# Scan of the delta rule: gathered rows in two buffers, TensorE's small products spread over VectorE's solution, products of the identity in what is left

## The reference, cut to what matters

```python
def step(M, inp):
    q_t, k_t, v_t, b_t = inp
    out_t = einsum('bnh,bnhd->bnd', q_t, M)
    retrieved = einsum('bnhd,bnd->bnh', M, k_t)
    delta = v_t - retrieved
    M = M + b_t[..., None, None] * einsum('bnh,bnd->bnhd', k_t, delta)
    return (M, out_t)
...
_, outs = jax.lax.scan(step, M0, xs)
...
rms = sqrt(mean(out * out, axis=-1) + EPS)
return (out / rms * rms_weight) @ Wo.T
```

## Time and profile before

| | |
|---|---|
| median of 3 runs | 2787.47 us (2787.09 to 2791.15) |
| the profiled execution's own time | 2809.05 us |
| its span, first to last instruction | 2807.4 us |
| mean granted TensorE clock | 0.925 of full speed |
| PE busy | 2337.0 us (83%) |
| DVE busy | 1622.4 us (58%) |
| ACT busy | 1364.7 us (49%) |
| POOL busy | 1143.1 us (41%) |

### The profile page before, as it was taken

How to read it: one execution, slowest core, us unless ns; L and a number is a source line. 1 busy time by engine, 2 the same in 40 slices (tenths; PEclk the granted TensorE clock), 3 DMA queues, 4 the chain that set the end, 5 groups by cost and what they waited for, 6 DMA issues and landing times. The chain is left out here.

```text
span 2807.4 us, 55147 instructions
## 1 busy us (share of the span) xinstructions
PE 2337.0 (83%) x20480; PEld 1593.8 (57%) x20480; DVE 1622.4 (58%) x4120; ACT 1364.7 (49%) x2098; POOL 1143.1 (41%) x1179
## 2 busy tenths in 40 slices
PE   5955566666999888888888887999789879999977
PEld 3534455555666454555455454676556756666666
DVE  4666777766113567767766763432254346877753
ACT  3531222222332386877787685533111347777752
POOL 3319999970001266646645653000076003223220
PEclk9977898877999899999999999999799989999999
DMA  4454445531101021111111111000000100000001
GB/s 147 150 147 147 140 137 156 155 110 52 37 1 36 29 66 48 59 44 54 57 56 39 52 51 46 0 1 0 2 1 1 36 0 1 1 1 1 1 1 60
DMA packets 158461, 149.00 MB, mean 53 GB/s; under 512 B 21169, under 2 KB 141105, under 8 KB 155121
## 3 DMA queue, kind: packets, MB, share of 16 engines
q1 hardware_dynamic: 138432, 105.51, 12.7%
q0 software_dynamic: 3456, 23.07, 2.4%
q10 hardware_dynamic: 16304, 16.83, 2.0%
HBM read 100.51 MB, written 40.63 MB: 50 GB/s over the span
## 5 line engine op out<-in xcount | busy, mean ns | idle before, releaser
L1633 POOL TENSOR_SCALAR a_dist<-a_dist,a_mq 128x512 f32<-128x512 f32 x512 | 354.9, 721 | 161.0 <-ACT a_mq L1572 161.0
L1676 DVE TENSOR_SCALAR_CACHE_REDUCE a_dist<-a_ring 128x512 f32<-128x512 f32 x512 | 332.3, 686 | 103.8 <-PE a_ring L1321 102.4
L1562 ACT ACTIVATE a_pT<-a_psT 128x1024 f32<-128x1024 f32 x256 | 257.9, 1023 | 123.6 <-PE a_psT L1333 116.5
L1333 PE MATMUL a_psT<-ident,a_dist 128*128 128x128 f32 x2048 | 276.2, 284 | 17.7 <-ACT a_pT L1562 17.6
L1333 PEld LDWEIGHTS a_psT<-ident,a_dist 128*128 128x128 f32 x2048 | 244.4, 146 | 50.6 <-issue 21.2
L1556 ACT ACTIVATE a_dist<-a_dist 128x2048 f32<-128x2048 f32 x128 | 237.0, 1902 | 61.5 <-DVE a_dist L1676 58.6
L1321 PE MATMUL a_ring<-a_stack 102*128 102x512 bf16 x512 | 190.3, 409 | 78.8 <-DVE a_dist L1676 42.4
L1321 PEld LDWEIGHTS a_ring<-a_stack 102*128 102x128 bf16 x512 | 48.5, 99 | 253.1 <-DVE a_dist L1676 174.7
L1002 POOL TENSOR_TENSOR c_y<-c_prod 128x1024 f32<-128x1024 f32 x16 | 37.2, 2349 | 335.6 <-DVE c_prod L1035 333.7
L3050 ACT ACTIVATE ds_wtm<-ds_wg,ds_par 128x256 f32<-128x256 f32 x64 | 29.0, 501 | 266.4 <-DVE ds_wg L3184 225.7
L1346 PE MATMUL a_psO<-a_pT,a_va 128*32 128x512 f32 x1024 | 143.9, 640 | 2.3 <-ACT a_pT L1562 2.3
(11 more groups left out here) (404 smaller groups left out, 5490.6 us busy)
## 6 DMA issues: line engine op xcount, KB each, us to landing
a_stack<-a_parts_dram SPq DMA_DIRECT2D x384, 64.0 KB
a_parts_dram<-a_parts SPq DMA_DIRECT2D x32, 384.0 KB, 2.5
bf_w<-in_up_w_dram POOLq DMA_DIRECT2D x10, 1024.0 KB, 5.8
bf_w<-in_down_w_dram POOLq DMA_DIRECT2D x10, 1024.0 KB, 6.9
ds_nbg<-tok_nbk ACTq DMA_DIRECT2D x128, 64.0 KB
X<-in_x_dram SPq DMA_DIRECT2D x2, 2048.0 KB, 11.1
feat_v<-di_part SPq DMA_DIRECT2D x16, 256.0 KB, 2.6
tok_nbk<-di_nbk SPq DMA_DIRECT2D x16, 256.0 KB, 2.9
```

Source lines behind the costliest of these rows:

```text
L1333: last = turn(psT[:, u % 2, kb, q * P:(q + 1) * P], dist[:, g % 2, i, q, k * P:(k + 1) * P], core.ident[:])
L1562: a(pT[:, u // 2, u % 2], psT[:, u % 2], ACT.Exp).then_inc(exp_done, 1)
L1633: last = nc.gpsimd.tensor_scalar(d, d, -1.0, mq[:, g % 2, i, q:q + 1], ALU.mult, ALU.add)
L1676: ts(dist[:, gg % 2, i, q, :], ps[:], 1e-12, 3.0e38, ALU.max, ALU.min, accum_out=mq[:, gg % 2, i, q:q + 1]).then_inc(ring_out, 1)
```

## The change: what it does

- nbg gets two buffers and two semaphores. ScalarE issues the load for chunk n + 1 in the middle of chunk n (after `root`), where it waits only for the previous chunk's products, which read that buffer.
- On TensorE `tile` moves ahead of `products` and waits for the sixth instruction of the solution; where there is no tile yet (j = 0), `fill(3)` stands there. `products` waits for the 14th. Behind L2966 comes a new `fill(3)` that waits for the 19th. `fill(3)` is three products of the identity with two copies of the identity (128 x 128 by 256 columns) into psX, which is written anew before it is read again.
- On ScalarE `take_out` moves ahead of the copies into pb, `tile_ready` ahead of `keys`, and `root` and the loads of nbg ahead of the load of qj.

```diff
+        PER = 3 * (CT // 2 - 2) + 4
-        nbg = sbf("nbg", [P, G, G, P])
+        nbg = sbf("nbg", [P, 2, G, G, P])
...
+            def fill(n):
+                for _ in range(n):
+                    mm(psX.rearrange("p j g t -> p (j g t)"), core.ident[:],
+                       core.ident[:].unsqueeze(1).broadcast_to([P, 2, P]), start=True, stop=True, skip_group_check=True)
...
                 last.then_inc(w_ps, 1)
 
+                ch.wait(pe, sol, PER, 4 + 6)
+                if ch.j:
+                    tile(Chunk(ch.j - 1, ch.pp, ch.u), 0, 0)
+                else:
+                    fill(3)
+
+                ch.wait(pe, sol, PER, 4 + 14)
                 if more:
                     products(ch.next())
-
                 ch.wait(pe, m2_done, 1, 1)
...
                 last.then_inc(o1_ps, 1)
 
-                if ch.j:
-                    tile(Chunk(ch.j - 1, ch.pp, ch.u), 0, 0)
+                ch.wait(pe, sol, PER, 4 + 19)
+                fill(3)
...
-                ch.wait(pe, nbg_in, 64, 64)
+                pe.wait_ge(nbg_in[ch.n % 2], 64 * ch.pair(1))
...
-                                      nbg[:, :, j, i * Q:(i + 1) * Q], start=False, stop=True, skip_group_check=True)
+                                      nbg[:, ch.n % 2, :, j, i * Q:(i + 1) * Q], start=False, stop=True, skip_group_check=True)
...
+                if ch.last():
+                    take_out(ch.last())
+
                 ch.wait(act, bl_done, 1, 1)
                 a(window(pb, 7, [[8, 6], [48, 13]]), ...
-                if ch.last():
-                    take_out(ch.last())
+                if ch.j:
+                    tile_ready(Chunk(ch.j - 1, ch.pp, ch.u), 0, 0)
 
                 if more:
                     if ch.u:
                         load_v(ch.pair(1))
                     keys(ch.next())
 
                 if ch.j:
-                    tile_ready(Chunk(ch.j - 1, ch.pp, ch.u), 0, 0)
+                    root(Chunk(ch.j - 1, ch.pp, ch.u), 0)
+                if more:
+                    ch.wait(act, m_ps, 2, 0)
+                    load_nbg(ch.n + 1)
                 if more and ch.u:
                     ch.wait(act, o1_ps, 1, 1)
                     load_qj(ch.pair(1))
-                if ch.j:
-                    root(Chunk(ch.j - 1, ch.pp, ch.u), 0)
-
-                if more:
-                    ch.wait(act, m_ps, 2, 2)
-                    load_nbg(ch.at(1, 1))
```

More of the change, by code:

```diff
@@ L2775, in delta_scan @@
             sem("kj_in"), sem("kx_in"), sem("qj_in"), sem("qx_in"), sem("ng_in"), sem("v_in"), sem("nbx_in"),
-            sem("nbg_in"), sem("qkx_in"))
+            [sem(f"nbg_in{n}") for n in range(2)], sem("qkx_in"))
         x_ps, q_ps, b_ps, w_ps, o1_ps, e_ps, m_ps, o_ps, y_ps = (
@@ L2873, in _ @@
             pool.wait_ge(nbx_in, 64)
-            pool.wait_ge(nbg_in, 64)
+            pool.wait_ge(nbg_in[0], 64)
             beside.run(nc, pool)
@@ L3011, in load_nbg @@
                 for g in range(G):
-                    act.dma_start(nbg[strip(g), g].rearrange("p i f -> p (i f)"),
-                                  nb_cols[c][g].unsqueeze(0).broadcast_to([2, CT, 512])).then_inc(nbg_in, 16)
+                    act.dma_start(nbg[strip(g), c % 2, g].rearrange("p i f -> p (i f)"),
+                                  nb_cols[c][g].unsqueeze(0).broadcast_to([2, CT, 512])).then_inc(nbg_in[c % 2], 16)
             def keys(ch):
@@ L3113, in _ @@
             dve.wait_ge(masks_in, 48)
-            PER = 3 * (CT // 2 - 2) + 4
             def solve(ch):
```

## The result

The changed kernel takes 2766.86 us (median of 4 runs, 2757.11 to 2767.04) against 2788.24 us of the kernel before (4 runs, 2787.09 to 2791.15). The ratio is 0.9913, 95% interval 0.989 to 0.9936: 21 us faster. 36.5 us were forecast; 2766.86 lies in the range 2742 to 2771, near its high end, and almost on rival 1's 2767.

A forecast was written before the change was run, and what follows sets the result against it. The scan was taken as bound by the chain VectorE - TensorE - VectorE, with TensorE's clock low. 46.5 - 5.5 - 3.5 - 1.0 = 36.5 us saved from 2787.5 gives 2751 us, range 2742 to 2771.

The forecast's parts named there:

- rival 1: TensorE's clock in the scan holds only in part, every chunk taking 14.03 us: saves 20.5 us, 2767 us; chance 0.16.
- What bounds the kernel: The scan is bound by the chain VectorE - TensorE - VectorE; TensorE's clock and a few waits can be won.
- Does the clock hold: Fills in the solution's pauses hold TensorE's clock except behind stalls; before, the tiles' chunks had 0.77, 0.92, 0.88, 0.80.
- Rival 3: Fills in the scan do not raise TensorE's clock and run at the low one: slower, 2805 us; chance 0.06.
- rival 2: Nothing changes on TensorE's clock, only the waits for nbg (2.4 us) and root (about 2) go: 2783 us; chance 0.06.
- TensorE's order: Beside the solution, the second fill ends at 372.0, aT comes at 372.30: 0.3 us to spare at full clock.
- The ceiling: All 31 scan periods at 13.22 us instead of 14.69 give 45.6 us, the last chunk's products 0.9; together 46.5.
- What does not go: Subtracted from the possible scan gain: 5.5 us for kx loads, 3.5 for low clock behind stalls, 1.0 for issue waits.
- Moving nbg's four DMA issues: Moving them (2.5 us of ScalarE's queue) into the solution costs nothing; only qj's loads stand behind, needed 10 us later.
- kx: Its loads made TensorE wait 6.6 us in two places, 0.54 each being usual: 5.5 us that the change leaves.
- Pauses named issue: TensorE's waits in the midst of groups, 11.6 us in seven places, mostly hidden before: taken to cost 1 us.
- The closing products: After the scan, three of eight tiles at low clock: may gain up to 3 us or nothing; taken as nothing.

The follow-up runs named there:

- a1: The changed kernel without both groups of identity products (fills); order, waits and buffers stay: 2800.68 us, ratio 1.0022 to the kernel before.
- c1: The changed kernel measured once more, with a second trace: 2771.25 us, ratio 0.9922 to the kernel before.
- c4: The kernel before, measured once more with a trace: 2794.16 us, ratio 0.9999.
- c2: The changed kernel with nbg's loads behind aT and those of qj, and ng's load ahead of qx: 2755.77 us, ratio 0.987 to the kernel before.
- c3: The changed kernel with nbg's loads behind aT and those of qj, and two products in the second fill: 2756.88 us, ratio 0.9871 to the kernel before.
- b2: The changed kernel with nbg's loads behind those of qj and behind aT, still two buffers: 2760.66 us, ratio 0.987 to the kernel before.
- b4: The changed kernel without the second fill, the one that waits for the 19th instruction: 2793.15 us, ratio 0.9984 to the kernel before.

## Why the prediction was right, and where its size was off

- **What bounds the kernel** was right: the chain, and in it TensorE's clock. a1 shows it from the other side, the same order at a clock of 0.78 is no faster than before.
- **Does the clock hold** was right in the main: 0.97 over the 31 periods (0.94 in c1) where it was 0.84 (0.80 in c4). The sign asked for was over 0.95 in each tile's window, and 0.95 and 0.94 in the first and third miss it narrowly. These products raise the clock (0.78 without them in a1). The rule of the Trainium skill ("TensorE: Matmul & The Clock Gate", Part 4) on transposes through the identity does not reach them. Rival 3 falls with that, and rival 2 too.
- **TensorE's order** was right to 0.2 us in the undisturbed chunk. The 0.3 us to spare ahead of L2994 were 0.15.
- **The ceiling** of 46.5 us stands: undisturbed periods have 13.24 us, of the forecast 13.22.
- **What does not go** was mis-sized, and this is the 15 us between the forecast gain and the measured one. I subtracted 10 us; the 31 periods alone hold 22.4 us in the first trace of the changed kernel and 447.2 - 409.8 = 37.4 us in the second. The step that failed is "Moving nbg's four DMA issues (2.5 us of ScalarE's queue) into the solution costs nothing". It counted ScalarE's queue and not what the 256 KB do to the transfers issued beside them. I had the contention in the text, for kx, and took "no change, because the bytes are the same". The bytes are; their issue moved from 12.8 us into chunk 11 to 6.3, where kx, qkx and qj are under way. With nbg loaded late again, c2 and c3 (each with one small edit more) are 15.5 and 14.4 us faster than c1, about what is missing; b2's ratio of 0.987 on 2788.24 would be 2752 us, an estimate, beside the forecast 2751.
- **How** the earlier nbg delays the copies stays open. The Trainium skill ("DMA: Bandwidth & Descriptors", Queues, rings and completion order) has each DMA engine take turns between the queues that hold work for it. That would fit qkx on SP's queue being late when nbg stands on ScalarE's, but no run tests it. Full engines alone do not explain it: 6 to 10 us into the chunks with u = 1 the DMA share is 0.42 to 0.48 in the changed kernel, and was 0.65 to 0.69 before (means over chunks 3 to 29).
- **kx** was mis-sized the other way. I took 5.5 us from two waits. The first of them (the line below, of the kernel before) lay ahead of the 31 periods: its products began 1.25 us behind the scan's first transpose (199.97), as in a chunk without a wait. Only some 1.3 us of the other one (1.86 us, usual 0.54) lay in the periods, and about as much in the changed kernel.

```profile
201.22 1.93 PE L2939 MATMUL ds_psB<-ds_kx,ds_wg 128*32 128x128 f32 x32 [4.72 <-DMA ds_kx<-feat_k]
```

- **Pauses named issue** I took at 1 us, since nearly all lay in L2894 and L2966. In the changed kernel the ones that cost time lay in L2936, on the chain itself, and in the fill: 4.5 and 0.9 us in three chunks, with the clock's fall behind them in two. What makes them is not shown.
- **ng**: the diff moves `products` behind the 14th instruction, and SP issues ng only behind qx, which waits for them. I had not followed that on SP's queue. In chunk 20 ng was issued at 490.4 and used at 500.9. Most of it is nbg's place again (2.4 and 3.4 us in b2 and c3 against 12.1 and 10.6), the swap takes the rest.
- **The closing products** I took at nothing within bounds of 0 to 3 us. They gave 3.4 us, 10.6 instead of 14.0. The last chunk ahead of them gave another 1.7, where 0.9 had been counted.
- **Rival 1's** time was the measured one by coincidence, not by its mechanism: the clock did not fall behind the 0.93 us pause between the tile's products and the next ones. It fell in five chunks, each time behind a pause of another kind: 2.53 and 1.91 us with a late ng, and 1.40, 1.86 and 0.64 us named issue, in the midst of a group. The 0.64 us are short; what tells them from the 0.93 us that the clock survived is not shown.

## What to carry to other kernels

Where a small-product engine sits in a chain, its clock is a term of the chain: work of no use laid into its pauses can pay, if it ends before the data that the chain waits for. How little is enough has to be measured: two products in the second fill kept the clock as three did (c3), none lost the gain (b4). A load that gets a second buffer gets a free choice of place; put it where no transfer that is soon waited for is issued beside it, not where its own wait happens to be met first. And follow each queue that waits for a moved instruction: here SP's loads hung on products that moved by 2 us.

## What the runs showed that I had not expected

- TensorE lost its clock behind short pauses: with pauses beside the solution of some 0.3, 0.9 and 1.7 us (b4) it ran at 0.84, with 0.3, 0.9, 0.3 and the fill it ran at 0.97.
- The attention stage, untouched by any edit, took from 726.9 to 750.9 us in fourteen traces, and single scans of one kernel differ by 12 to 15 us. One pair of traces gave 51.9 us for a change of 21.
- The kernels with nbg behind aT (b2, c2, c3) move the same bytes in the same number of transfers as the changed kernel, in shorter scans than c1's, and waited 3.5 to 6.3 us for the copies to qkx instead of 12.0 and 25.2.
